# Attention and feed-forward block on one core: weights loaded in pieces, a split last pair and shorter scale chains

## The reference

```python
Q = layernorm(x) @ wq; K = ctx @ wk; V = ctx @ wv          # 16 heads of 16
corr = irfft(rfft(Q) * conj(rfft(K)))                       # over the positions
top_vals, top_idx = top_k(corr, 4);  w = softmax(top_vals)
out = sum over i of w[i] * V rolled in the head's channels by top_idx[i]
x = x + out @ wo
```

```python
W_in_q  = round(W_in  * 127 / amax per hidden channel)      # also for W_out
x_q     = round(xn * 32767 / max(abs(xn)))                  # xn = layernorm(x), one scale for all
hidden  = gelu(x_q @ W_in_q + b_in)
h_q     = round(hidden * 32767 / max(abs(hidden)))          # one scale for all
x = x + h_q @ W_out_q + b_out
```

## Time and profile before

| | |
|---|---|
| median of three runs | 1082.83 us |
| time of the profiled execution itself | 1082.9 us |
| its span, first to last instruction | 1081.1 us |
| outside the span | 1.8 us |
| attention steps 0 to 3 end at | 45.04 us |
| last output projection of the attention starts at | 592.78 us |
| first layer of the feed-forward | 602.88 to 825.25 us |
| second layer | 830.23 to the end |

### The profile page before, as it was taken

How to read it: one execution, slowest core, us unless ns; L and a number is a source line. 1 busy time by engine, 2 the same in 40 slices (tenths; PEclk the granted TensorE clock), 3 DMA queues, 4 the chain that set the end, 5 groups by cost and what they waited for, 6 DMA issues and landing times.

```text
span 1081.1 us, 29028 instructions
## 1 busy us (share of the span) xinstructions
PE 1056.0 (98%) x9358; PEld 780.6 (72%) x9358; DVE 968.9 (90%) x2790; ACT 937.4 (87%) x1698; POOL 504.6 (47%) x674
## 2 busy tenths in 40 slices
PE   7899999999999999999998899999998999999998
PEld 5688888888888888888886344444444888888886
DVE  3788888888888889888898899999997999999998
ACT  4699999998888888888888688888888999999996
POOL 4688888888888888888887300000000000000000
PEclk9999999999999999999999999999999999999999
DMA  7333445334434333333331498999999899999995
GB/s 227 91 119 119 119 121 142 123 119 126 122 111 131 119 119 118 119 119 119 118 119 50 144 333 304 303 297 303 304 303 363 319 344 336 349 335 347 340 344 198
DMA packets 141425, 222.59 MB, mean 206 GB/s; under 512 B 72320, under 2 KB 92160, under 8 KB 137216
## 3 DMA queue, kind: packets, MB, share of 16 engines
q1 hardware_dynamic: 140224, 220.12, 61.7%
q10 hardware_dynamic: 1088, 1.05, 0.3%
HBM read 121.00 MB, written 83.89 MB: 190 GB/s over the span
## 4 chain that ended last, share of the span: by engine, by line
PE 73%; DVE 12%; issue 9%; ACT 2%; DMA 1%; DVEq 1%; POOL 1%; ACTq 0%; POOLq 0%
PE bank L606 20%; PE bank L437 8%; PE bank L450 7%; PE bank L512 7%; PE bank L488 7%; DVE arena L1442 7%; PE bank L462 6%; PE bank L500 5%; PE bank L474 5%; PE bank L527 5%; DVE arena L1435 2%; DVE arena L1457 1%; PE bank L637 1%; ACT arena L900 1%; DMA arena<-in_ctx_turned 1%
## 5 line engine op out<-in xcount | busy, mean ns | idle before, releaser
L637 PE MATMUL bank<-wout,arena 128*128 128x256 f16 x2048 | 235.5, 273 | 2.9 <-DVE arena L1435 0.9
L637 PEld LDWEIGHTS bank<-wout,arena 128*128 128x128 f16 x2048 | 195.6, 98 | 44.5 <-DVE arena L1442 13.2
L606 PE MATMUL bank<-arena,win 128*128 128x512 f16 x1024 | 221.3, 379 | 1.0 <-DVE arena L1393 0.9
L606 PEld LDWEIGHTS bank<-arena,win 128*128 128x128 f16 x1024 | 100.0, 98 | 122.4 <-issue 1.4
L1442 DVE SCALAR_TENSOR_TENSOR arena<-arena,wout_rel 128x512 f16<-128x512 int16 x256 | 183.1, 746 | 3.8 <-ACT arena L900 1.3
L857 ACT ACTIVATE arena<-bank,b_in_sb,z_scale 128x512 f32<-128x512 f32 x192 | 146.9, 777 | 15.1 <-PE bank L606 10.1
L723 ACT ACTIVATE arena<-arena 32x128 f32<-32x128 f32 x256 | 78.6, 307 | 50.7 <-DVE arena L1172 48.4
L657 ACT ACTIVATE arena<-bank 128x512 f32<-128x512 f32 (+1 forms) x196 | 115.2, 590 | 8.0 <-PE bank L437 4.6
L657 ACT ACTIVATE arena<-arena 128x512 f16<-128x512 f32 x192 | 112.9, 618 | 3.8 <-DMA arena<-in_ctx_turned 3.2
L893 ACT ACTIVATE arena<-arena,one 128x1536 int16<-128x1536 f32 x64 | 100.2, 1568 | 18.3 <-DVE arena L1442 15.4
L1407 DVE TENSOR_REDUCE hmax<-arena 128x1 f32<-128x1024 f32 x96 | 111.3, 1211 | 2.9 <-ACT arena L857 2.9
(11 more groups left out here) (125 smaller groups left out, 2074.4 us busy)
## 6 DMA issues: line engine op xcount, KB each, us to landing
hidden_scratch<-arena SPq DMA_DIRECT2D x32, 1536.0 KB, 5.6
arena<-hidden_scratch SPq DMA_DIRECT2D x64, 768.0 KB, 6.8
arena<-in_ctx_turned SPq DMA_DIRECT2D x64, 256.0 KB, 2.6
arena<-in_x_turned SPq DMA_DIRECT2D x64, 256.0 KB, 2.8
arena<-in_x SPq DMA_DIRECT2D x64, 256.0 KB, 3.8
x_scratch<-arena SPq DMA_DIRECT2D x64, 256.0 KB, 3.6
arena<-x_scratch SPq DMA_DIRECT2D x32, 512.0 KB, 5.9
out<-arena SPq DMA_DIRECT2D x32, 512.0 KB, 3.8
```

The source lines that it names most:

```text
L606: last = nc.tensor.matmul(bank[f][:, :].rearrange("p (n t) -> p n t", n=4), win16[:, f, c, :], xt[q % 3][:, s, :, c, :], start=s == 0 and ...
L637: last = nc.tensor.matmul(bank[m * 2 + k // 2][:, k % 2 * D:(k % 2 + 1) * D], gbuf[:, s, f, k * P:(k + 1) * P], wout16[:, f, :], start=f = ...
```

## The change

- The constants of the inverse DFT (128 KB) are loaded by SP behind the loads of step 1, no longer ahead of step 0. The output weight `wo` (256 KB) is issued by ScalarE at the end of step 1; its high and low halves are made in step 2, no longer in step 1.
- `W_in` and `W_out` are loaded in eight pieces of two chunks (256 KB), one behind the loads of each of steps 4 to 11; the two biases in step 12.
- VectorE takes the maxima of one chunk a step, in steps 10 to 17 for `W_in` and 19 to 26 for `W_out`; the scales are made in steps 18 and 27. ScalarE rounds the weights in steps 20 to 43; the transpose of `W_in` is issued in step 36.
- For the last pair, the second sequence's output goes to bank 7. VectorE makes the residual and the statistics of the first sequence before the second is there (`last_residual`). ScalarE normalizes the first sequence only, and VectorE the second; each gets its own maximum (`last_magnitude`).
- The last maximum of the hidden values is taken in two halves, the first one after the last gelu but one.
- The clip takes the multiplication by 1/32767 with it, so that the reciprocal is the scale: one single-column operation less in front of each rounding; two more operations on scales are merged.

```diff
@@ -28,7 +28,8 @@
 FINISH_AFTER = {4: 0, 6: 1}
-W_STEP = 4
+W_LOAD = 4
+W_STEP = 10
 AHEAD = 5
@@ -139,8 +140,9 @@
         b_out_sb = sb("b_out_sb", [P, D], F32)
-        xmax = sb("xmax", [P, PAIRS], F32)
-        hmax = sb("hmax", [P, QUADS, FC // 2], F32)
+        xmax = sb("xmax", [P, PAIRS + 1], F32)
+        hmax_all = sb("hmax_all", [P, QUADS * FC // 2 + 1], F32)
+        hmax = hmax_all[:, 0:QUADS * FC // 2].rearrange("p (q k) -> p q k", q=QUADS)
@@ -304,7 +306,6 @@
             sp.dma_start(cst[:, :], table).then_inc(S["const_in"], 16)
-            sp.dma_start(inv16[:, :, :, :], inv_table).then_inc(S["direct_in"], 16)
@@ -316,13 +317,16 @@
                 if t == 1:
-                    sp.dma_start(w_in_raw, w_in.rearrange("(c p) d -> p c d", p=P)).then_inc(S["w_in_loaded"], 16)
-                if t == 2:
-                    sp.dma_start(w_out_raw, w_out.rearrange("(c p) n -> p c n", p=P)).then_inc(S["w_out_in"], 16)
-                if t == 3:
+                    sp.dma_start(inv16[:, :, :, :], inv_table).then_inc(S["direct_in"], 16)
+                c = 2 * (t - W_LOAD)
+                if 0 <= c < FC:
+                    sp.dma_start(w_in_raw[:, c:c + 2], w_in.rearrange("(c p) d -> p c d", p=P)[:, c:c + 2]).then_inc(S["w_in_loaded"], 16)
+                if FC <= c < 2 * FC:
+                    sp.dma_start(w_out_raw[:, c - FC:c - FC + 2], w_out.rearrange("(c p) n -> p c n", p=P)[:, c - FC:c - FC + 2]).then_inc(S["w_out_in"], 16)
+                if t == W_LOAD + FC:
                     sp.dma_start(b_in_sb[:, :], b_in.rearrange("(c p) -> p c", p=P), allow_slow_non_contiguous=True).then_inc(S["b_in_in"], 16)
                     sp.dma_start(b_out_sb[:, :], b_out.rearrange("(a n) -> a n", a=1).broadcast_to([P, D])).then_inc(S["b_out_in"], 16)
-                if t == W_STEP + 16:
+                if t == W_STEP + 26:
                     sp.wait_ge(S["w_in_staged"], FC // 2)
@@ -509,8 +513,10 @@
                         for k, (i, j) in enumerate(PARTS):
-                            last = nc.tensor.matmul(pair(0)[:, b, :], ot16[p % 2][:, i, c, b, :], w16[:, j, 2, c, :],
+                            last = nc.tensor.matmul(pair(7)[:, 1, :] if p == PAIRS - 1 and b == 1 else pair(0)[:, b, :], ot16[p % 2][:, i, c, b, :], w16[:, j, 2, c, :],
                                                     start=c == 0 and k == 0, stop=c == DC - 1 and k == 2)
+                    if p == PAIRS - 1 and b == 0:
+                        last.then_inc(S["y_half"], 1)
                 last.then_inc(S["y_done"], 1)
@@ -656,8 +662,12 @@
-            for n, w in ((3, wk), (0, wq), (1, wv), (2, wo)):
+            def load_w(n, w):
                 nc.scalar.dma_start(w_attn_raw[:, n, :, :], w.rearrange("(c p) n -> p c n", p=P)).then_inc(s_w_in[n], 16)
+            load_w(3, wk)
+            load_w(0, wq)
+            load_w(1, wv)
@@ -725,7 +735,7 @@
                 act.wait_ge(S["scales_done"], p + AHEAD + 1)
-                for b in range(2):
+                for b in range(1 if p == PAIRS - 1 else 2):
                     last = nc.scalar.activation(xnt[:, p, b, :], x1[p % 2][:, b, :], ACT.Identity, bias=nm[p % 2][:, b, :], scale=rs[p % 2][:, 0, b, :])
@@ -767,7 +777,7 @@
             def weights(t):
-                k, r = (t - W_STEP) // 3, (t - W_STEP) % 3
+                k, r = (t - W_STEP - 10) // 3, (t - W_STEP - 10) % 3
                 if 0 <= k < 4:
@@ -804,6 +814,8 @@
                 if t == 1:
+                    load_w(2, wo)
+                if t == 2:
                     high_w(2)
@@ -1070,7 +1082,7 @@
-                V.tensor_reduce(top_[:, 2 * k:2 * k + 2], raw[:, 2 * k:2 * k + 2, :], AX_X, ALU.max, apply_absolute_value=True).then_inc(S["w_scale_chain"], 1)
+                V.tensor_reduce(top_[:, k:k + 1], raw[:, k, :], AX_X, ALU.max, apply_absolute_value=True).then_inc(S["w_scale_chain"], 1)
                 chain[0] += 1
@@ -1095,15 +1107,17 @@
-                if t == 2:
-                    dve.wait_ge(S["w_in_loaded"], 16)
-                    for k in range(4):
-                        largest_w(w_in_raw, win_max, k)
+                n = t - W_STEP
+                if n == 0:
+                    dve.wait_ge(S["w_in_loaded"], 16 * FC // 2)
+                if 0 <= n < FC:
+                    largest_w(w_in_raw, win_max, n)
+                if n == FC:
                     scales(win_max, win_up).then_inc(S["w_in_scaled"], 1)
-                if t == 3:
-                    dve.wait_ge(S["w_out_in"], 16)
-                    for k in range(4):
-                        largest_w(w_out_raw, wout_max, k)
+                    dve.wait_ge(S["w_out_in"], 16 * FC // 2)
+                if FC < n <= 2 * FC:
+                    largest_w(w_out_raw, wout_max, n - FC - 1)
+                if n == 2 * FC + 1:
                     link(scales(wout_max, wout_up))
@@ -1195,6 +1209,21 @@
+            def last_residual():
+                p = PAIRS - 1
+                dve.wait_ge(s_x1_st[p % 2], p // 2 * 16)
+                dve.wait_ge(S["xn1_done"], p - 1)
+                dve.wait_ge(S["y_half"], 1)
+                V.scalar_tensor_tensor(x1[p % 2][:, 0, :], pair(0)[:, 0, :], 1.0 / W_UP, xin[p % UNROLL][:, 0, :], ALU.mult, ALU.add).then_inc(S["x1_half"], 1)
+                dve.wait_ge(S["x1_half"], 1)
+                dve.wait_ge(S["ln2_stats"], p)
+                V.bn_stats(st2[:, 0, :], x1[p % 2][:, 0, :])
+                dve.wait_ge(S["y_done"], p + 1)
+                V.scalar_tensor_tensor(x1[p % 2][:, 1, :], pair(7)[:, 1, :], 1.0 / W_UP, xin[p % UNROLL][:, 1, :], ALU.mult, ALU.add).then_inc(S["x1_done"], 1)
+                dve.wait_ge(S["x1_done"], p + 1)
+                V.bn_stats(st2[:, 1, :], x1[p % 2][:, 1, :]).then_inc(S["x_chain"], 1)
             def moments2(p):
@@ -1207,6 +1236,16 @@
                 V.tensor_reduce(xmax[:, p:p + 1], xnt[:, p], AX_XY, ALU.max, apply_absolute_value=True).then_inc(S["xmax_part"], 1)
+            def last_magnitude():
+                p = PAIRS - 1
+                dve.wait_ge(S["scales_done"], PAIRS + AHEAD)
+                V.tensor_scalar(xnt[:, p, 1, :], x1[p % 2][:, 1, :], rs[p % 2][:, 0, 1, :], nm[p % 2][:, 1, :], ALU.mult, ALU.add).then_inc(S["xn1_last"], 1)
+                dve.wait_ge(S["xn1_last"], 1)
+                V.tensor_reduce(xmax[:, PAIRS:PAIRS + 1], xnt[:, p, 1, :], AX_X, ALU.max, apply_absolute_value=True)
+                dve.wait_ge(S["xn1_done"], PAIRS)
+                V.tensor_reduce(xmax[:, p:p + 1], xnt[:, p, 0, :], AX_X, ALU.max, apply_absolute_value=True).then_inc(S["xmax_part"], 1)
@@ -1269,7 +1308,7 @@
                     low_w(0, 2)
-                if t == 1:
+                if t == 2:
                     low_w(2, 3)
@@ -1352,11 +1391,10 @@
             moments2(PAIRS - 2)
-            residual(PAIRS - 1)
-            statistics2(PAIRS - 1)
+            last_residual()
             moments2(PAIRS - 1)
             magnitude(PAIRS - 2)
-            magnitude(PAIRS - 1)
+            last_magnitude()
@@ -1373,9 +1411,8 @@
             then(V.tensor_reduce(one[:, 0:2], bank[5][:, 0:2 * P].rearrange("p (k j) -> p k j", k=2), AX_X, ALU.max))
-            then(V.tensor_scalar(x_amax, x_amax, TINY, None, ALU.max))
-            then(V.reciprocal(x_up, x_amax))
-            V.tensor_scalar(x_up, x_up, INT16, None, ALU.mult).then_inc(S["x_scale"], 1)
+            then(V.tensor_scalar(x_amax, x_amax, TINY, 1.0 / INT16, ALU.max, ALU.mult))
+            V.reciprocal(x_up, x_amax).then_inc(S["x_scale"], 1)
             dve.wait_ge(S["x_scale"], 1)
@@ -1395,13 +1432,18 @@
             round_x(0)
-            then(V.tensor_scalar(z_scale[:, :], win_max[:, :], x_amax, 1.0 / INT8, ALU.mult, ALU.mult))
-            V.tensor_scalar(z_scale[:, :], z_scale[:, :], 1.0 / INT16, None, ALU.mult).then_inc(S["x_scale"], 1)
+            V.tensor_scalar(z_scale[:, :], win_max[:, :], x_amax, 1.0 / INT8, ALU.mult, ALU.mult).then_inc(S["x_scale"], 1)
             then(V.reciprocal(wo_topr, wo_top))
...
                 for k in range(FC // 2):
+                    if q == QUADS - 1 and k == FC // 2 - 1:
+                        dve.wait_ge(S["b_gelu"], q * FC + (FC - 1 + FC))
+                        V.tensor_reduce(hmax_all[:, QUADS * FC // 2:], kept[:, q, 0, :], AX_X, ALU.max, apply_absolute_value=True)
+                        dve.wait_ge(S["b_gelu"], q * FC + (FC + FC))
+                        V.tensor_reduce(hmax[:, q, k:k + 1], kept[:, q, 1, :], AX_X, ALU.max, apply_absolute_value=True).then_inc(S["b_max"], 1)
+                        continue
                     dve.wait_ge(S["b_gelu"], q * FC + (2 * k + 2 + FC))
@@ -1416,14 +1458,12 @@
             dve.wait_ge(S["b_max"], QUADS * FC // 2)
-            V.tensor_reduce(hm_part, hmax[:, :, :], AX_XY, ALU.max).then_inc(S["hmax_part"], 1)
+            V.tensor_reduce(hm_part, hmax_all[:, :], AX_X, ALU.max).then_inc(S["hmax_part"], 1)
             dve.wait_ge(S["hmax_all"], 1)
```

(8 more changed lines are left out.)

## The result

The changed kernel takes 1077.85 us, the median of six runs (1076.11 to 1079.57); the kernel before took 1082.78 us in six runs beside it (1080.44 to 1085.17). The ratio is 0.9955, with a 95% interval of 0.9939 to 0.9971: 4.9 us faster. The forecast was 1074.5 us with a range of 1072.5 to 1078.2 us. The profiled execution took 1077.55 us, with a span of 1075.8 us, 5.3 us less than before.

The account below looks back on a forecast made before the run. TensorE, busy 98% of the span, bounds the kernel; gains lie where it idles or is slow. Start 6.6 + loop 0 + last pair 1.1 + last gelu 0.7 = 8.4 us, so 1082.9 - 8.4 = 1074.5 us; range 1072.5 to 1078.2 us.

Parts of the forecast that it names:

- rival 1: Steps 1 to 3: wo lands late or a ScalarE wait is missed, only 4.4 us gained, 1076.7 us; chance 0.12.
- rival 4: Steps 1 to 3: a new TensorE gap halves the clock and costs 2.0 us again, 1076.5 us; chance 0.05.
- rival 2: Loop: x arrives late, VectorE has no slack for the added maxima, up to 7.9 us lost, likely 1078.5 us; chance 0.09.
- signs of being wrong: A loop step over 8.95 us, ScalarE waiting for wo, or K projections that start at 26 us again.
- The start: Steps 1 to 3: moved loads and weight work let step 4 begin at 38.4 us, 6.6 us earlier; bounds 4.4 and 8.0 us.
- The replay: Steps 1 to 3: engines' operation lists rerun with profiled lengths from the context landing at 16.2 us.
- The loop: Steps 4 on: moved loads, maxima and scale operations cost 0; bounds a gain of 0 and a loss of 7.9 us.
- the cover: Loop: ScalarE's wait for turned roll weights, 0.8 us a step, hides a late VectorE; without it 0.4 us a step lost.
- The last pair: Before the first feed-forward layer: residual 0.25 us, normalizing and maxima 0.7 us, one scale link 0.19 us, together 1.1 us.
- The link: Scale chain before the first feed-forward layer: one operation goes, 601.20 to 601.39 us, 0.19 us gained.
- The last gelu: Before the second feed-forward layer: halved last maximum gains 0.5 us, one scale operation less 0.19 us, together 0.7 us.
- Rival 3: Loop: weight pieces collide with loads, 1.26 us in each of eight steps, 10.1 us lost, 1084.6 us; chance 0.04.

Follow-up runs that it names:

- port_reduce: Kernel after with one more unused VectorE tensor_reduce of 128x8, SBUF to SBUF, at the end of each of steps 30 to 45; 1078.52 us, single run.
- whole_loads: Kernel after with W_in loaded whole behind the loads of step 4 and W_out behind those of step 8, instead of eight pieces; 1076.77 us, single run.
- wo_slot: Kernel after with wo's high half made by ScalarE ahead of the copy of the DFT of Q in step 2; 1075.70 us, single run.
- pool_late: Kernel after with wo's high half earlier in step 2, maxima and chains ahead of x's statistics, POOL's output bias chain after the third input rounding; 1073.62 us.
- early_slot: Kernel after with the weights' maxima and scale chains on VectorE ahead of the statistics of x, not at the step's end; 1074.29 us, single run.
- tail_only: Kernel before with only the last pair by sequence, the halved last maximum and the merged scale chains; 1080.29 us, ratio 0.9981.

## Why the prediction was right where it was, and where it was not

The side and the range were right, the middle was 3.35 us too low: 4.9 us came of the 8.4 us forecast. That the time still lies in the range, 0.35 us below its end, is partly luck. The upper part of the range was made for rivals 1, 4 and half of rival 2, and what filled it was in part a wait that no rival names. Of the prediction's own signs of being wrong one came: steps of the loop over 8.95 us. By its steps:

- **The start** was right in mechanism, and against this profile in size: 6.84 us for 6.6 us. The replay gave 19.9, 21.7, 30.1 and 38.4 us for the DFT of Q in step 1 and the begins of steps 2, 3 and 4; the trace has 19.77, 21.75, 29.91 and 38.20 us. It also held for the two runs that moved wo. The size was met in part by chance, since the old start ended at 45.04 us in one profile and at 43.71 us in another. The clock stayed at 1.00, so rival 4 did not come, nor did rival 1.
- **The loop** is the step that failed: "I put the loop at 0". It cost 3.2 us. The sixteen maxima of 0.40 us did cost nothing, as forecast, apart from 0.08 us in step 14. But the two chains of small operations were put at 0.6 and 0.9 us, and took 1.76 and 1.75 us (162.46 to 164.22 us, and 243.54 to 245.29 us): in each, two operations waited for POOL. And the cover was overrated. The 0.8 us of ScalarE's wait are not TensorE's slack; TensorE loses what the four maxima come late beyond 0.45 us, and the free time ahead of the late x cannot be used by work that stands behind it. Rival 2 named the place and the late x, but with 0.4 us in each of sixteen steps as its price, where two steps lost 1 to 2 us each. In the run port_reduce the late x cost 0.36 us in step 47, in which VectorE had no new work at all.
- The kernel before had shown it. These are its scale chains of steps 2 and 3:

```profile
26.23 0.17 DVE L1081 TENSOR_SCALAR win_up<-win_up 128x8 f32<-128x8 f32 x1
...
33.83 1.17 POOL L976 TENSOR_TENSOR arena<-arena 128x512 f16<-128x512 f32 x1
...
34.75 0.28 DVE L1079 TENSOR_SCALAR wout_max<-wout_max 128x8 f32<-128x8 f32 x1
```

  The same form took 0.17 us with POOL idle, and 0.28 us where POOL's operation ended at 35.00 us, the VectorE one at 35.03 us. In steps 1 to 3 POOL was idle for a third to a half of the time; in the loop it is busy 7.7 of 8.89 us. A small operation moved from the one into the other has another price.
  The Trainium skill says this ("SBUF — State Buffer", section "Who interferes with whom"): VectorE and GpSimd share a second pair of SBUF ports, a lock that is held for a whole instruction; tensor_scalar and copies can take it, an operation with two SBUF inputs contends with GpSimd's reads, and on Trainium2 tensor_reduce never does. By that section it is the order of issue, not the shape, that decides who waits. Beside POOL's tensor_tensors the runs agree: 878 ns against 144 ns in the median, 0.16 us by way of PSUM, 1.69 against 0.69 us. Beside a tensor_scalar of POOL they do not: in the kernel before, the rounding of the earlier trace rows (601.39 us, 0.81 us) began within this operation and ended 0.25 us ahead of it:

```profile
601.18 1.27 POOL L1041 TENSOR_SCALAR store_x<-store_x,cst 128x256 bf16<-128x256 bf16 x1
```

- **The last pair** gave 0.98 us for 1.1 us. The part up to the last POOL scale gave 0.36 us (4.60 us instead of 4.96 us; forecast 0.25). From its end (593.75 us) to the maximum over all (595.01 us) it took 1.26 us, forecast 1.15 us, instead of 1.88 us: 0.62 us. Its tensor_scalar took 0.41 us instead of 0.3. The link gave 0.18 us. Then 0.18 us was lost, which the forecast does not have: the first rounding took 1.00 us, 0.81 us before. In whole_loads and wo_slot the same tail took 8.88 us, and the rounding 0.75 us, although it starts 0.01 to 0.02 us behind a POOL operation there as in after.
- **The last gelu** gave 0.73 us for 0.7 us, and the filling matmuls ended just before the transpose, as forecast.
- **Rival 3** did not come: neither pieces nor 1 MB at once cost the loop anything. The Trainium skill's advice to batch transfers ("DMA: Bandwidth & Descriptors", Bandwidth) was neither confirmed nor refuted by the time; whole, W_in landed in 5.6 us, and in pieces in 3.4 us each, but TensorE waited for neither.

What stays open: why VectorE waits 0.7 us for x in one step and 1.8 us in another, and so how much each run loses; what moving the constants of the inverse DFT gave; and why the rounding is held up in after and not in wo_slot, from nearly the same start.

## What to carry to other kernels

The price of an operation belongs to its place: before moving a small VectorE operation, look at what POOL does there, and if POOL is busy, give it a PSUM side or another form, or a place where a wait hides it. Free time in an engine that works in order can only be used by what stands ahead of the wait; put the movable work in front of the load's wait, not at the end of the step. And slack is to be read to the engine that bounds: how late an operation may come before TensorE waits is another number than how long the next engine waited for it.

## What the runs showed of the hardware

- A VectorE tensor_scalar from SBUF to SBUF waits for the POOL tensor_tensor of 128x512 under way, however small it is: up to 1.11 us for eight columns. The three of sixteen that took 0.15 us without such a wait began within 0.02 us of the start or the end of a POOL operation. With one side in PSUM, and as a tensor_reduce, it takes 0.14 to 0.17 us beside POOL.
- POOL's tensor_scalar of 128x256 does not hold it up to its end. The rounding of 128x1024 takes 0.75 us alone (pool_late). Begun 0.21 us into that operation in the kernel before it took 0.81 us, and begun 0.16 us into it in early_slot 0.85 us.
- When the two start together, either can be slowed. POOL's operation takes 0.95 us beside a VectorE tensor_reduce (pool_late). In the kernel after it took 1.27 us and the rounding 1.00 us, in wo_slot 1.55 us and 0.75 us:

```profile
595.06 1.55 POOL L1053 TENSOR_SCALAR store_x<-store_x,cst 128x256 bf16<-128x256 bf16 x1
595.08 0.75 DVE L1428 TENSOR_SCALAR arena<-arena,one 128x1024 int16<-128x1024 f32 x1
```

- Two gaps of TensorE of nearly the same length had different ends. After 2.58 us in the kernel before (at 40.09 us) the clock stayed full: the next eight matmuls of `attend` took 1.06 us. After 2.50 us in tail_only they took 1.92 us, and the granted clock of that step was 0.86; there TensorE had had two shorter gaps, of 1.74 and 1.64 us, in the two steps ahead, in the kernel before one of 3.46 us.
